# Four chained cross-attention layers on one core: another hand-laid order for five engines, and 111 products of constants on TensorE in the last pairs

## The reference

```python
# layer 0: 8 heads of 64 channels, keys and values from the context
x = x + Wo @ attention(Wq @ norm(x) + bq, Wkv @ context + bkv) + bo
# layer 1: 16 heads of 16, masked keys from layernorm(context)
x = x + tanh(gate) * (attention(x @ Wq.T, a @ Wk.T, a @ Wv.T) @ Wo.T)
# layer 2: keys from the context and from x itself, then rmsnorm and a gelu MLP
x = x + mlp(rmsnorm(attention(...) @ out_w + out_b + x))
# layer 3: self-attention, cross-attention, MLP, each on a layernorm, with residuals
x = x + attention(ln1(x)) @ w_ao + b_ao
x = x + attention(ln2(x), context) @ w_co + b_co
x = x + gelu(ln3(x) @ w1 + b1) @ w2 + b2
```

## Time and profile before

| | |
|---|---|
| median of 3 runs | 1304.58 us (1303.95 to 1304.62) |
| the profiled execution's own time | 1303.31 us |
| its span, first to last instruction | 1301.4 us |
| TensorE busy | 1238.8 us (95%) |
| VectorE, ScalarE, GpSimd busy | 1026.2, 869.2, 565.5 us |
| mean granted TensorE clock | 0.987 |

### The profile page before, as it was taken

One profiled execution on the slowest core, in us unless ns is written; L12 is line 12 of the kernel. 1 busy time (PEld: TensorE's weight loads), 2 busy tenths in 40 slices (PEclk: granted clock), 3 DMA queues, 4 the chain that ended last, 5 costly groups with the idle time before them and its releaser, 6 DMA issues.

```text
span 1301.4 us, 35231 instructions
## 1 busy us (share of the span) xinstructions
PE 1238.8 (95%) x13116; PEld 963.6 (74%) x13116; DVE 1026.2 (79%) x2452; ACT 869.2 (67%) x2287; POOL 565.5 (43%) x977
## 2 busy tenths in 40 slices
PE   6999999999999999999999999999999999999775
PEld 4766778777777877777786777868777787868554
DVE  4778887888978787888878788787888888696753
ACT  3666677776767777776766776768676777766441
POOL 2553454264444526345344535443354453442321
PEclk9999999999999999999999999999999999999896
DMA  8100000000000000000000000000000000000000
GB/s 323 35 18 19 2 24 3 22 8 7 18 11 19 7 22 8 18 7 11 19 7 22 8 6 19 12 18 7 23 8 6 19 7 6 3 6 2 6 5 5
DMA packets 23589, 25.78 MB, mean 20 GB/s; under 512 B 10624, under 2 KB 22912, under 8 KB 23168
## 3 DMA queue, kind: packets, MB, share of 16 engines
q1 hardware_dynamic: 23424, 23.55, 5.8%
HBM read 21.44 MB, written 2.10 MB: 18 GB/s over the span
## 4 chain that ended last, share of the span: by engine, by line
PE 79%; DVE 9%; issue 5%; ACT 4%; POOL 2%; DMA 0%; SPq 0%; POOLq 0%; DVEq 0%; ACTq 0%
PE bank L687 10%; PE bank L953 8%; PE bank L513 8%; PE attended L642 8%; PE bank L627 7%; PE bank L962 7%; PE bank L693 5%; PE bank L721 5%; PE bank L502 4%; PE bank L747 4%; PE bank L710 3%; PE bank L734 3%; PE bank L680 2%; PE bank L421 2%; PE bank L738 2%
## 5 line engine op out<-in xcount | busy, mean ns | idle before, releaser
L614 POOL TENSOR_SCALAR p_a<-p_a,rec_a 128x256 f32<-128x256 f32 x512 | 244.3, 495 | 187.7 <-DVE rec_a L569 187.5
L600 ACT ACTIVATE p_a<-bank,nmax_a 128x256 f32<-128x256 f32 x512 | 236.8, 476 | 68.2 <-DVE nmax_a L563 67.5
L563 DVE TENSOR_REDUCE nmax_a<-bank 128x2 f32<-128x512 f32 x256 | 167.8, 678 | 12.6 <-PE bank L513 11.8
L627 PE MATMUL bank<-ident,p_a 128*128 128x128 f32 x1024 | 143.0, 277 | 5.6 <-POOL p_a L614 2.7
L627 PEld LDWEIGHTS bank<-ident,p_a 128*128 128x128 f32 x1024 | 114.2, 142 | 33.6 <-issue 25.2
L513 PE MATMUL bank<-k_a,q_a 64*128 64x256 f32 x1024 | 137.5, 395 | 1.2 <-ACT q_a L580 0.7
L642 PE MATMUL attended<-p_a,v_a 128*64 128x256 f32 x1024 | 133.7, 390 | 2.6 <-DVE v_a L474 1.1
L513 PEld LDWEIGHTS bank<-k_a,q_a 64*128 64x128 f32 x1024 | 92.4, 186 | 27.6 <-issue 18.8
L600 ACT ACTIVATION_READ_ACCUMULATOR p_a<-bank,nmax_a 128x1 f32 x512 | 106.0, 207 | 0.0
L642 PEld LDWEIGHTS attended<-p_a,v_a 128*64 128x64 f32 x1024 | 64.1, 136 | 55.2 <-issue 21.9
L675 ACT ACTIVATE p_a<-bank 128x512 f32<-128x512 f32 x128 | 75.8, 602 | 29.6 <-PE bank L627 28.9
(11 more groups left out here) (260 smaller groups left out, 2987.1 us busy)
## 6 DMA issues: line engine op xcount, KB each, us to landing
wb<-in_wb SPq DMA_DIRECT2D x1, 4096.0 KB, 12.3
wc<-in_wc SPq DMA_DIRECT2D x1, 4096.0 KB, 24.8
xc<-in_x SPq DMA_DIRECT2D x16, 128.0 KB, 2.7
xc<-in_ctx SPq DMA_DIRECT2D x16, 128.0 KB, 2.9
c_top<-in_ctx SPq DMA_DIRECT2D x16, 128.0 KB, 2.7
k_c<-in_ctx SPq DMA_DIRECT2D x16, 128.0 KB, 2.1
res_a<-in_x SPq DMA_DIRECT2D x16, 128.0 KB, 2.2
out<-y_out SPq DMA_DIRECT2D x16, 128.0 KB, 1.7
```

Of the source, the lines that this page charges most:

```text
L563: dve.tensor_reduce(nmax_a[:, n, e, :], ps[:, :].rearrange("p (q k) -> p q k", q=KT), AX.X, ALU.max, negate=True).then_inc(A.s["max"], 1)
L600: last = act.activation(p_a[:, j % 2, n, e, qt, :], ps[:, qt * D:(qt + 1) * D], ACT.Exp, bias=nmax_a[:, n, e, qt:qt + 1], accum_out=sum_a[ ...
L614: last = pool.tensor_scalar(p_a[:, j % 2, n, e, qt, :], p_a[:, j % 2, n, e, qt, :], rec_a[:, n, e, qt:qt + 1], 1.0, ALU.mult, ALU.mult)
L627: last = nc.tensor.transpose(ps[:, kt * D + qt * P:kt * D + (qt + 1) * P], p_a[:, j % 2, n, e, qt, kt * P:(kt + 1) * P], ident[:, :])
```

## The change

All five order strings and `BANK` are replaced by others of the same steps: on TensorE 378 of 1492 steps stand at another place in the string (the new products not counted), on ScalarE 251 of 1121, on VectorE 715 of 2374, on GpSimd 105 of 706, on SyncE 13 of 114; most have moved by one to three places. No step is added or taken away, apart from a new stage `w` on TensorE: 111 steps, each one product of two constants, `ident` (as weights) by `mean_of_all`, 128 columns, into `attended_bank`, which after the last pair's `x1` nobody reads. The first of them waits for that `x1`.

```diff
@@ -47,6 +47,7 @@
 BANKS = 7
 AHEAD = 4
+IDLE_WORK = 111
...
@@ -95,84 +96,85 @@
 ORDER = {
     "sp": (
-        "nsksbkfednbkfebfedkdnbndebdenkfbydnefkdbnyekfdbnyekfbdynekfbdnyekfdbnyekfbdynekfbdynekfybdnefkybndekfybednkfyf"
+        "nksskbdefnkbdebfefkdnbndebdenkfbydnefkdbnyekfdbnyekfbdynekfbdnyekfdbnyekfdbynekfbdynekfybdnefkybndekfybednkfyf"
...
     "pe": (
-        "nsnknnakaaaaaddaadddddaadsddkddkaankdndddkskksddaadkkdaadkdadddnnaabddbdnadbdddaanddbdbdbaddkkbdaeddeeeededddd"
+        "nksnnnaakaaaaddaadddddaakdkkddnksddddkknaaddskksddaaddaadkdadddnnaabddbdnadbdddaanddbdbdbaddkkbdaeddeeeededddd"
...
-        "ndddbaaafdddgfgkgfkkgkkkbkgaakdbdbddbhdcbdcccehceeeehdadcdcacdhedchddddfddfeefeedebbefffgkkfkgkgkbkkkggbbhbchc"
-        "cbcehceeeehehcccceeeeefeffggggffgfkfccchchchhhccccfffffffhhhhh"),
+        "ddnbdfaaagdddfgkgfkkgkkkbkgaakdbdbddbhdcbdcccehceeeehdadcdcacdhedchddddfddfeefeedebbefffwwwgkkfkgkgbkggkkkbbhb"
+        "wwchccbcecheeeehehcccwwwwwwwwwwwwwwwwwceeeeewwwfweffwwgwwwggwwwgffgfkfcwwcchchchhhwwwwcccwwwwwwwcwwwwwwwwwwfww"
+        "wfwfwwwwwwwwwwwwwwwwwwwwwwwwwwwwfffwwwwwwwfwwwwwwwwwwhwwwhhwwhh"),
...
@@ -1232,6 +1234,15 @@
+        def pe_w():
+
+            pe = nc.tensor
+            for n in range(IDLE_WORK):
+                yield
+                if n == 0:
+                    pe.wait_ge(A.s["x1"], A.at(PAIRS, "x1", 0))
+                mm(attended_bank[:, 0:P], ident[:, :], mean_of_all[:, :], start=True, stop=True)
+
...
@@ -1413,7 +1424,7 @@
-                weave("pe", {"s": [pe_s()], "n": all_pairs(pe_n), "a": all_pairs(pe_a), "d": all_pairs(pe_d), "k": all_pairs(pe_k),
+                weave("pe", {"s": [pe_s()], "w": [pe_w()], "n": all_pairs(pe_n), "a": all_pairs(pe_a), "d": all_pairs(pe_d), "k": all_pairs(pe_k),
```

More of the change, by code:

```diff
@@ new lines @@
+        "nksnnnaakaaaaddaadddddaakdkkddnksddddkknaaddskksddaaddaadkdadddnnaabddbdnadbdddaanddbdbdbaddkkbdaeddeeeededddd"
+        "adadananeebeebaaenakekddddnadbdgaggbbdggbdabcddcceceeceededdddaaaddccdadcdeedaceeadefddfefnandbddbdaafdafndfdk"
+        "kkdnfagkkkkkgbgaddghgbddbcabcccbhcehdeeehecddcdecaaddadcdddhaddfannefbeeeadbeaaendddanddgdadgfgddggadffdfdaadd"
+        "fdckacckkcdckkkadbkkdddcddchaabcbdbcaabhebfdeeeedbehfnnddhheeaeeaedfedddnddaddagaadggddndffgfgkdddfkdkdaadkkkc"
+        "kbcdcckhdcbbabanhbbchencdeeeedaecdhbcadhdeeeeaeadnfeanfdddaddgfddggaaddggffddafckkkcccfkkdbdddcddahkkbkbabhhbc"
@@ new lines @@
+        "dceaeeeehebddbdahcnnaeeceeaedndfeadndfdgddafddggaaddggffafddkkdcafkcckkkcbdkcakdddhdbdbabhhbcaeheeeedenanchddd"
+        "bacbeecdeendeadfeafnddafddgaddggafddfgddgfaakkkfcddddkkkkkcbccddaahdbcdbaabhbhecceeeencendchddhdabeebeedeaaend"
+        "dfdnadfdaddfdgdaagdgdadggffadfckfkkcckkkcbaahkkdddhhabdbhdbcddbheddeeeecbcdaebcnnaacddeedfdefaefddnaedddaaefdf"
+        "ddfnkkkdgfkggkkggbdkdaakcddhdcabcbcdbchbdeheeeeccaebcahbddhceaeeednefanefadfddgddggaagndgdffddfnakkkfdddcdkkhc"
+        "cbkkcchhbabkhhbddbccaacaeceeeedddedaadddadffebedbeedaenneafdddagnagdddgfgfgnfddfckkkccchkkchhbkhkdhakdbddbcabc"
@@ new lines @@
+    "act": (
+        "knnaakaaasadaadaaadaaakdakadkaadkkaaaadaadaaadnnabadbaaadbabdabbaabdaakdeaaeddaeanenaeebaeebaaaeaakaddaagbbgbb"
+        "gdaabcaadecedcdeaacccaaaaeceeddaeeaefaanandbdfbfafafaafadkkkgaakkggbabdahbbcabachedhccecdccaaaaeddeaafnnaeabee"
+        "eadbeaadaagadaagdgffffaafdaadcakaakkckackcddcbchbbcbaabaaaebfaadehbhnedeneeeeaaaeddaafgaafdaaggffafadkdkkdaakc"
+        "kbcbhbbabacncabachenhcdeacdbeeeeeeaaeaafaadadaagdfggafadaffaafckkkckddbahbkbbcbacahcechaaebdbdaecneneeeeaeafaa"
+        "adgdaafggfaadffaafdaakckakkckbabddhbbcbaachcheaaenanceddbecbeeeeaaefaaadadgafaafgfgfaaddfaaakkkcdkkcbadbhbaaba"
+        "baaccecchhencndedebeebeeaeaaaadfdaaaadgaafdggfaaaffafckkkkchakabdbdahabbahbdeccdecbcaabcnneeaeefaeadeaadefadaf"
+        "affdafkkkgaaggkkdbbcaadhbabacbheccheccacbaaebdeeeeedaanefaanagdfggfaadaffafakkkacddkhkcbbhbhbaaccbccaaceaaedde"
+        "adafaeebedaeeabaeannadgafafgdfgafafckkkchkhchckbbdabdabcbcaaceeddaafeneneeeebaeabaadagadagaagafddfffaafckakkac"
+        "khkbbhhdbdbccbcacaecaaeaaeddeeefeeaeaaaadnnabagbfdfgfgfaafkkkckcbkdbdhbacbcbcaachecaadaadaaehdfedeaeeeeaefaafn"
+        "aabafdnbdfaagaafagkgkkkkbbadbbdabhcaacehecdccdcaachaaeddfeeeeeebfbffffgkkkggkbbkbbhbchcehceccceceeeeeefgfgfgff"
@@ L147 @@
[L147 to L157 removed]
+        "nnnknknknsnsknnnnnnaaaaaaasdaaaadaaaaaaafbenkdnakadnannsnadkkkknaaknnndaanassaaadaakaadadaannaadnanaandnnnaabb"
@@ new lines @@
+        "bbbdbbabnbabbdbaaannnnabaadkabbaadaeeeeeeeeeeededaeaeenadeeanenaaanaaaenannnaaeegkgkgdgdagnkknabbbbbnbbnbbgbba"
+        "gbaangcccabdcaabdbcaceecccceeeceeeceeeceeaadccaccdaaceeaaeacedeacafffdfaaaedafeegffffgnafnffkffafnfafdndaaagng"
+        "nnganafdnfnfaahkhnhnakhnkkkkgbbbbbgbbababdbbgbcacccaacbcabbhccccchccececcceceeeddeeeeeaaecaaeacefdfdfefaaheead"
+        "aeannfnanaeaaenengndngagagdngannnnaaadagffffagfdfffkfgffafaccccafaadafaadfhhhchcaacccckcckacbbccbkcbbcbbcbbdbb"
+        "kdabakcdkaacbfafffbbaaaaheeaeeeedeeeeeheefeeneedenaahnnaaeffffeegfdgngdgaafgnknaanfaffaafafgfaagndadnnnnfagccc"
@@ new lines @@
+        "cffhdhhhaadkkbbbbbcbbcbbkkbbkcbckccdacacbcacacaccbchbnahneneneeeedaeeeeeceeceefeefehfaadfaaaennnanaeegagngafgd"
+        "ngnaadannffffafkfggfaadfffffaagacdcccaafccffhkhhhbbbbbdbcbcbbckbbcbckkcdckakbacachccbchbdaaaeeeeeeaeeeeedeeahe"
+        "eceennecnfafnfafedaananenegngggaangfdnnndnaffffafkfgafgffafadffaagaccccaaadfaaffhhchchkkbbbbbbcbcbbkkccbkbkbac"
+        "dcacacbchaccdcbhabaeeaeeeedeeeeenneeheedecencenafaafdfnnfaenanaeeggggaafgdnaffffadkfaffaafgfgfafaafdnnnndagccc"
+        "faacaaffhhhhdkkkkkckbbbbbcbbdbbabbabaccccdaacacbcaccbbccachheeeeeenceeeeeneeceedeefenhanfdfafeaaaeengngnangagd"
@@ new lines @@
+        "nagafdnnnaaanffffdaaaffkgfgffafaadffaagcccacfffhhhchckkbbbbbabbakkdkbkaahbahbbbdaaccbccdcbbcchcdeeccceeceedaae"
+        "eeeeceenecnfafefaafeenednaafaaffffdakfnffaenaffnfaafeefgndgagdgnaagfannnnffhkhahghgkgcbbcbcbbcbbabakkbkbbkdbda"
+        "cacabcccchcbbccdchcecceceeeeaeeeeeaeeceeaeecefdfafaahfnaeaaneegafggngadgffffkfdfgfgnffaaffnfnnnaagadccccanfaan"
+        "nnnffhdhhdhkaccbbbbbkbbcbcbhbbcbchcaackkckckachccbcbbaacaacfefafeeeeedfeeeeedeaeaeedeaaeaeadfdaaaenaneegggagff"
+        "ngffnkfaffafgfnffdfaganadnngncaccfcnffhnhnhnchckcccchcchbbcbbbcbbcbhckabkbbabkddckcakaabacbbcfeffefeeeedeeeeed"
@@ new lines @@
+        "eeaeefeedennnaanaeaaaeegngngngnaagndaadnnnngaaagfffffkafafdffgffcfcdaaccaafacffhchhakhkkkbbbbbcbkbkbhbhcbccbdc"
+        "bccdchcbccacabbaaaceeaeeeeceeeeefeefefefeeaeaddaaefaaaeegggagaffffgdnnafafkfnffngffdgfananandnafgccncncnnnffhk"
+        "hhchcbbbbbkbcbcbbccbbcbcackcckcacbcadkdkhbbaaaceaaacfefdfaaahfeeaeedeeeeeeedehefeedffeffakfaffaaefdfaaaneegfga"
+        "afgfndggaadaaaaafggffhhhhkkbbbbbbbgbcabcbbkkbacdkcdkbaaabbacchcccceecceececcecchcaaddcaaaeeeeecefafhfefeedefed"
+        "ffffekfdffeffffefgeggggfffhhhhgkgbbbbbbbbgbkbbcbckccbhccbcccchcececeeecceceeceeeceeheceeeceffffeegfggggffffffg"
@@ new lines @@
+        "ffgffffgcccfcffhhhhcchcccchcccchccccccfffffffffffffffffffhhhhhhh"),
+    "pool": (
+        "ssknaaaaaaaakakaaaknkaaaaaaaaaaakanbabaaaaegaaaekeeaaaaaagnaabbccaaegacaeccaaccaaeeffaaaakfkfffaagaanhkhaakcbc"
+        "baacaeagcceccaaffaaeeaaaganaakffaakcffcaaaahhcaackckccbbaaffeagaeaaeeaakfkfgaaaafaanfaacchhkkcbcbcaaeccgaaefee"
+        "faaaangaakfkaaffaacfcaachkhckcbbeccgaaeaaeeffaagaankfkfaaffaaccaaaahhckkccbbaaeccgeaafeefaagaankkffaaaaffaacca"
+        "ahhkkcbbccaaaaegccefeefaaaagnaakfaakfaaffaacchhckkaabbaaccegeccfaafeeaakkffaaaaffgaanhkhaakccbbcaaccegeccaaeef"
+        "faaaagkkffffaaccaanhhkaackcbbcaaccegfaefaaaeeaaaakgkfffaafcacanhhckcckbbcacaaeagffeeeaagaanaakfkfaacffcaahchak"
+        "akccbbccegaaeaaffeeaakgafkfafaafaacnchkhckccbbcceagaaafeafaaakkfeefaaaaffgaaaahhkkcbbcaaegaaccceccaafafakkfeef"
+        "ffghhkckbbccegcceccfeefgkffffcchhcccccffffffhh"),
@@ L174 @@
-    "302654130254613610325461302541302541360316310263102546310254631025460361032453045306142506342510632450163245016324"
-    "506312450631245063124506312450631250163245106324510632451032645103264510326451032645103")
+    "012345601423560142356014213456506215430654306542301654320134016235401623542630152463015302150436215043623165231046"
+    "351240632541062354106253146025360310316403125641203415204315624315630156320415021653402165340261534026514032032651"
+    "043160245630261034526103452610435614123023564120341526401352640135264310526431250643125064132504135240135240351240"
@@ new lines @@
+    "531420653105461302546103254625164260345123645012364503612450234520632140653214065321406251346213035304635210541052"
+    "160342516032451602365430613205461320546130254601302153103154362015436201543620153462015346203154602532015643210546"
+    "312054631205436201620135406524310264315042613504261235610253461025364102536412035643614236140562310452604321604521"
+    "460512460315412564120431204563120456314562301415604152316540213546021354062134501456214632016435012360413260413260"
```

(9 more changed lines are left out.)

56 lines of the change are left out of this document (2 added, 54 removed).

## The result

The changed kernel takes 1294.15 us (median of 6 runs, 1292.60 to 1297.57) against 1304.26 before; the ratio is 0.9924, 95% interval 0.9910 to 0.9938, some 9.9 us less. The prediction of 1300.7 us had the direction; the size lies beyond its range of 1295.5 to 1304.5. The profiled execution is the fastest of the six, 1292.60 us with a span of 1290.9.

A forecast was written before the change was run, and what follows sets the result against it. TensorE was taken as the bound from 60 to 1160 us, handoff latency at the end. Gains of 3.1 - 0.2 + 1.0 = 3.9 us from the 1304.58 us median gave 1300.7 us, range 1295.5 to 1304.5.

The forecast's parts named there:

- the term for the order in the bulk: 60 to 1160 us, start included: new order gains 1.0 us, only the 14.7 us of pauses can change.
- The prediction's own sign of being wrong: 60 to 1160 us: the same steps needing over 3 us more or less than 1100 us means the order decided.
- The last 40 us: End of kernel: full clock wins back 5.1 us, products beyond idle time cost 2.0, net 3.1 us gained.
- The excess ahead of c15.8: Last 40 us: 7 products take 1.57 us against 0.93 idle, so the step comes 0.64 us late.
- f15.3: Last 40 us: 28 products ahead of this step take 6.27 us against 6.03 idle, making it 0.24 us late.
- The stretch from 1176 to 1262 us: Products priced from 1176 to 1246 us: 0.2 us lost, between 1.5 gained and 4 lost.
- The products ahead of g14.0 and c14.0: From 1176 us: 3 and 2 products where TensorE works without a pause make it 1.1 us late.
- The scores of c14: Stretch from 1176 us: c14.4 placed ahead of h13.2 brings them 1.8 us earlier, 0.7 after the loss.
- The 17 products: Ahead of c14.8: 3.8 us against 1.85 idle, step 2.0 us late, 3 if the clock is still down.
- That the products don't hold the clock: Rival, cold stretches at the end: products cost 16.8 to 22.6 us, no clock won back, about 1323 us; chance 0.05.
- That the order brings more: Rival, bulk: order removes a third of the 14.7 us of pauses, 4.9 us, about 1296.5 us; chance 0.18.
- That the excess eats the gain: Rival, tail: c14.8 is 4 us late, the 3.1 us gain becomes about nothing, 1303.5 us; chance 0.22.

The follow-up runs named there:

- new_bulk: New orders and banks up to some 1160 us, the kernel before's orders from there, no constant products: 1300.81 us, ratio 0.9972.
- products_alone: The kernel before, old order and banks, with the 111 constant products ahead of the same steps: 1301.40 us, ratio 0.9979.
- fitted: The changed kernel with 116 constant products placed anew by the idle times its trace shows: 1290.66 us, ratio 0.9888.
- fitted_start: `fitted` with 29 more constant products in the pauses of the first 30 us, 13 ahead of the first weights' product: 1288.10 us, ratio 0.9871.

## Why the prediction fell short

**The bulk (predicted 1.0 us gained, start included; measured 5.0 in the profiled executions, some 3.7 in the runs of `new_bulk`).** This is the step that failed: the term for the order in the bulk, taken from "only the 14.7 us of pauses can shrink or grow" and put at 1.0 us. The prediction's own sign of being wrong, over 3 us more or less for the steps from 60 to 1160 us, came in with 5. The gain stayed below 14.7 us, but only 2.1 of it came out of the idle time; 2.9 came out of time that is shown as busy, which I had held to be fixed. The idle column is no bound on what TensorE loses. A matmul's shown end lies behind the point at which the next could have begun (eight transposes back to back start every 0.11 us and the last shows 0.27), so a wait of up to 0.16 us shows as busy and a longer one as less than it is. Measured from each step's start to the next's, against the tenth percentile of the same step with the same kind of neighbour in both traces, the bulk lost 59.8 us before and 55.2 after, while the floor is the same (1039.3 and 1039.6). Of that, waits over 0.2 us went from 41 to 31 and from 21.2 to 17.0 us. How high the level comes out hangs on what is held alike: with the kind of the step before held fixed as well it is 22 and 16 us. The difference, 4 to 7 us, and a floor that falls by 0.3 us at most come out either way. That is an estimate from the two traces and tells where the time went; why the new order waits less at just these places no run isolates. I also had no row for the sign of it, and took a small number because none could be summed. The Trainium skill ("Perfetto Trace Analysis", "Identifying the Most-Contended Engine") warns that matmul occupancy is no good measure of how far TensorE is from its peak, since its instructions are pipelined. These traces agree that it is none: TensorE was shown busy for 98.7% of the bulk before, and the same matmuls are busy for 1085.3 us in one and 1082.4 in the other, both at full clock.

**The last 40 us (3.1 predicted, 4.2 measured).** The mechanism held in each step. The excess ahead of c15.8 was 0.47 us where I had 0.64, since the products start behind the last transpose's issue and not its shown end, and the same at f15.6; f15.3 came 0.26 late (0.24) and h15.3 some 0.5 (0.45). The rest I had under-counted: the reciprocals' transposes L738 at 0.25 us, which I left out, and 0.25 more in L721, where both groups now run through.

**The stretch from 1176 to 1262 us (0.2 lost predicted, 1.4 gained measured).** The products ahead of g14.0 and c14.0 cost 0.8 us net, not 1.1. The scores of c14 came 1.79 us earlier against that, as forecast (what c14.4 passes is one MLP step of 16 instructions, not two); by the o step c14.7, 0.6 of it was lost again. The 17 products made c14.8 only 0.8 us late and not 2.0. They ran at full clock and took 3.96 us, near the 3.8 I had. What differs stands ahead of them: the wait inside the o step went from 1.38 to 0.69 us, and the two transposes behind it cost 0.4 less at full clock. That VectorE's earlier work shortened the wait is likely, but no run isolates it. Behind it, c14.8's own product gained 1.0 us and the transposes of e15 another 0.8 by the clock, 1.8 where my sum left room for 1.1. `products_alone` shows the other case: with the old order, where the clock is down for 3.4 us under the same 17, c14.8 is 2.9 us late, as I had put it for that case, and the stretch loses 1.9 us.

**The rivals.** That the products don't hold the clock is refuted: of the nine kernels that have products in short and long pauses from 1160 us on, the changed one among them, eight show a granted clock of 1.00 there up to TensorE's last matmul, and only `products_alone` has one fall of 3.4 us. That the order brings more was the right rival, at a chance of 0.18 and with 4.9 us. That it met the 5.0 us of the traces so closely is luck: it had them from a third of the idle time, which shrank by 2.1 us only. That the excess eats the gain is refuted, and `fitted` shows it was real all the same, some 3 us.

## What to carry to other kernels

When the last pieces of a pipeline leave TensorE idle in many short pauses, fill all of them with products of constants into a bank nobody reads, not only the long one: here that was worth 4.2 us of the last 40, and the same at the start, while the weights load, 2.8 to 4.0 more by step times (2.6 in the medians of `fitted` and `fitted_start`, whose intervals overlap). Count them against each pause as the trace shows it, put them ahead of the wait and not behind it (inside a step and for a bank too), and leave them out where none is idle. And don't take the idle time of a busy TensorE for what a better order can gain: count from start to start.
